# Change of phase in a one-core graph layer: key maximum, returning key rows and weight splits moved around the last tile

## The reference, cut to what matters

```python
xn = layernorm(x)
# graph part: msg[e] = (xn[src[e]] @ W[rel[e]]) * norm[e], summed by dst
# attention part, linear: k is softmaxed over the nodes
k = softmax(xn @ Wk, axis=nodes);  context[h] = k[h].T @ v[h];  out = q @ context
gate = sigmoid(gelu(LN(xn) @ Wg1 + bg1) @ Wg2 + bg2)
x = x + graph + (out * gate) @ Wproj + bproj
# mixture of experts: router, top 2 of 8, w1, gelu, w2
x = x + moe(layernorm(x))
```

## Time and profile before

| | us |
|---|---|
| median of 3 runs | 1686.28 (1685.11 to 1686.80) |
| the profiled execution | 1684.39 |
| its span in the trace | 1682.7 |
| PE busy | 1600.7 (95% of the span) |
| DVE, ACT, POOL busy | 1342.4, 964.2, 1007.7 |

### The profile page before, as it was taken

How to read it: one execution, slowest core, us unless ns; L and a number is a source line. 1 busy time by engine, 2 the same in 40 slices (tenths; PEclk the granted TensorE clock), 3 DMA queues, 4 the chain that set the end, 5 groups by cost and what they waited for, 6 DMA issues and landing times.

```text
span 1682.7 us, 31746 instructions
## 1 busy us (share of the span) xinstructions
PE 1600.7 (95%) x10509; PEld 1449.3 (86%) x10509; DVE 1342.4 (80%) x3389; ACT 964.2 (57%) x2156; POOL 1007.7 (60%) x1111
## 2 busy tenths in 40 slices
PE   7999999899899999998789999999999999999998
PEld 6888888778787777877689999999999999999998
DVE  7888565577677777776569999999999999999985
ACT  4444322345455554554566667667666767676764
POOL 4533322767666667664766766666767767776730
PEclk9999999999999999999899999999999999999999
DMA  9776656677677777778633333333333333333320
GB/s 302 262 259 244 235 226 238 222 250 247 226 254 258 245 240 242 252 240 294 209 95 101 105 102 112 101 108 101 116 102 105 101 115 100 107 99 114 104 62 10
DMA packets 127076, 290.50 MB, mean 173 GB/s; under 512 B 21271, under 2 KB 49724, under 8 KB 126914
## 3 DMA queue, kind: packets, MB, share of 16 engines
q1 hardware_dynamic: 86068, 177.19, 28.9%
q0 software_dynamic: 39952, 110.13, 23.7%
q10 hardware_dynamic: 894, 1.16, 0.2%
HBM read 149.49 MB, written 138.90 MB: 171 GB/s over the span
## 4 chain that ended last, share of the span: by engine, by line
PE 61%; DVE 13%; ACT 8%; issue 8%; another core or an unknown queue 5%; POOL 3%; DMA 1%; DVEq 0%; POOLq 0%; ACTq 0%
PE bank L1805 47%; DVE ml L1590 3%; ACT mh L1026 2%; PE bank L2008 2%; PE bank L1849 2%; DVE xres L1720 2%; DVE ht L1706 2%; POOL raw L691 2%; PE bank L1850 2%; PE bank L2009 2%; ACT raw L1082 2%; PE bank L1860 1%; PE bank L1960 1%; POOL stg L809 1%
## 5 line engine op out<-in xcount | busy, mean ns | idle before, releaser
L809 POOL DMA_INDIRECT stg<-table,idxcur x495 | 538.6, 1088 | 257.0 <-issue 179.4
L1805 PE MATMUL bank<-wreg,xt 128*128 128x512 f32 x2352 | 589.1, 400 | 8.3 <-issue 7.5
L1805 PEld LDWEIGHTS bank<-wreg,xt 128*128 128x128 f32 x2352 | 437.7, 191 | 101.3 <-issue 12.0
L691 POOL DMA_INDIRECT raw<-table,idxa x297 | 304.4, 1025 | 147.9 <-issue 90.1
L1805 PE MATMUL bank<-tt,wreg 128*128 128x256 f32 (+1 forms) x2400 | 318.6, 282 | 1.2 <-DVE tt L1656 1.2
L1805 PE MATMUL bank<-wreg,ht 128*128 128x256 f32 x2352 | 314.7, 282 | 0.5 <-DVE ht L1706 0.2
L1805 PEld LDWEIGHTS bank<-tt,wreg 128*128 128x128 f32 x2400 | 295.6, 189 | 4.2 <-issue 1.5
L1805 PEld LDWEIGHTS bank<-wreg,ht 128*128 128x128 f32 x2352 | 292.6, 188 | 1.7 <-issue 0.8
L1082 ACT ACTIVATE raw<-bank,cols 128x256 f32<-128x256 f32 (+1 forms) x400 | 164.9, 464 | 122.7 <-remote 70.8
L1219 DVE COPY stg<-bank 128x512 f32<-128x512 f32 x196 | 134.5, 687 | 126.1 <-PE bank L1805 88.1
L1590 DVE SCALAR_TENSOR_TENSOR ml<-stg,nrm,mh 128x256 fp32r<-128x256 f32 x455 | 196.0, 480 | 13.8 <-ACT mh L1026 13.8
(11 more groups left out here) (244 smaller groups left out, 2159.6 us busy)
## 6 DMA issues: line engine op xcount, KB each, us to landing
table<-stg SPq DMA_DIRECT2D x196, 512.0 KB
kv_d<-kvs SPq DMA_DIRECT2D x49, 256.5 KB
xt_d<-xt SPq DMA_DIRECT2D x49, 256.0 KB
xtp<-xt_d SPq DMA_DIRECT2D x24, 512.0 KB
stg<-table,idxcur POOLq DMA_INDIRECT x495
sk<-kv_d SPq DMA_DIRECT2D x24, 256.5 KB
out_x<-xres SPq DMA_DIRECT2D x24, 256.0 KB
xres<-in_x POOLq DMA_DIRECT2D x23, 256.0 KB, 3.8
```

The lines of the kernel that those rows point to most:

```text
L691: pool.indirect_dma_start(ring_a[:, r * EARLY + j, :], None, table[0:LIMIT, :], bass.IndirectOffsetOnAxis(ap=idxa[:, at:at + 1], axis=0)). ...
L809: pool.indirect_dma_start(stg[:, (s % 4) * SUP + j, :], None, table, bass.IndirectOffsetOnAxis(ap=idxcur[:, at:at + 1], axis=0)).then_inc( ...
L1805: mm = pe.matmul(dst, stat(a, c), mov(b, c), start=(n == 0), stop=(n == 3 * chunks - 1))
```

## The change

Six things change, all around tile 48 and pairs 0 and 1.

1. The turning, reducing and spreading of the key maximum is moved into tile 48 (`last_maximum` on DVE, a transpose at j = 7 on PE). The held tiles are shifted and exponentiated ahead of `first_phase_over`.
2. Parts 2 to 5 of the returning rows are loaded by SP in the middle of tile 48's stores; `later` then covers relation matrices already read. The parts are used in the order 2, 3, 4, 5, 0, 1, three of them in slot 0.
3. `wreg` is laid out by chunks, HI and LO of a chunk side by side, and chunks 4 and 5 go to the two places that `later` does not cover (`place_of`).
4. The chunks are split in slots (0,2), (0,3), (0,6), (0,7) by ACT and (0,3), (0,4), (0,7), (1,1) by DVE; before it was (0,7), (1,0), (1,2), (1,3) and (0,7), (1,0), (1,4), (1,5).
5. The end of the context is moved from slots 5 and 6 of pair 0 to slots 3 and 4. `OUT` and `GATES` of the first output pair move to the end of slot (0,7), and the rest of that pair's steps come one slot earlier in pair 1 (`SLOTS_OF_SECOND`).
6. The experts' products wait for the weight chunk that they read, in place of one wait for all.

```diff
+        weights = sb("wreg", [P, 4, 2, CC, WC, C], F32R)
+        wreg = weights[:].rearrange("p n h c r o -> p h n c r o")
...
+        def place_of(n):
+            return n if n < 4 else (n + 2) % 4
...
             def stores(k, i, b):
...
+                    if at(k, NT - 1) and h < 2:
+                        if h == 0:
+                            sp.wait_ge(kv_st[0], 16 * (NP + 1))
+                            sp.wait_ge(kv_st[1], 16 * NP)
+                        sp.wait_ge(gnn_mm, 8 * k + 2 * h + 2)
+                        load_rows(2 + 2 * h)
+                        load_rows(3 + 2 * h)
...
             load_rows(0)
             load_rows(1)
             first_phase_over(sp)
-            for part in range(2, 2 * GROUPS):
-                load_rows(part)
...
-                if (i, s) == SPLITS[0]:
+                if (i, s) == SPLITS[2]:
                     act.wait_ge(ctx_mm, HELD + REST)
...
+            def last_maximum():
+                dve.wait_ge(setup_pe, 4)
+                dve.wait_ge(gnn_mm, 8 * (NT - 1))
+                dve.wait_ge(xt_st[1], 16 * NP)
+                ch.link(dve, dve.tensor_reduce(kcol, bank[1][:, 0:C].rearrange("p (c n) -> p c n", c=CC), AX.X, ALU.max))
+                for c in range(CC):
+                    dve.tensor_scalar(dg[:, c * P:(c + 1) * P], ident[:], kcol[:, c:c + 1], None,
+                                      ALU.mult).then_inc(k_shift_diag, 1)
+            def held_shifts():
+                dve.wait_ge(kv_st[0], 16 * (NP + 1))
+                dve.wait_ge(kv_st[1], 16 * NP)
+                for b in range(HELD):
+                    dve.tensor_tensor(kvs[b][:, 0:C], kvs[b][:, 0:C], dg[:], ALU.subtract).then_inc(k_shift, 1)
...
+            dve.wait_ge(kmb_mm, 1)
+            ch.link(dve, dve.tensor_copy(dg[:], bank[1][:, C:2 * C]))
+            held_shifts()
+            dve.tensor_tensor(fade, kcol1, kcol, ALU.subtract).then_inc(k1_dve, 1)
+            keep_contexts(NT - 1, NP, 0, 7)
+            keep_contexts(NT - 1, NP, 1, 0)
             dve.wait_ge(flag_ready, 1)
             far = dve.value_load(flag[0:1, 0:1], min_val=0, max_val=NT * P * R)
             first_phase_over(dve)
...
+                    if at(k, NT - 1) and j == 7:
+                        pe.wait_ge(kmax_up, NT)
+                        for c in range(CC):
+                            mm = pe.transpose(bank[1][:, c * P:(c + 1) * P], kmax[:, c * P:(c + 1) * P], ident[:])
+                        mm.then_inc(setup_pe, 1)
...
-                if isinstance(i, int) and (i, s) == (0, 5):
+                if isinstance(i, int) and (i, s) == (0, 3):
                     context_turn()
                     context_values()
-                if isinstance(i, int) and (i, s) == (0, 6):
+                if isinstance(i, int) and (i, s) == (0, 4):
                     query_context()
+                if isinstance(i, int) and (i, s) == (0, 7):
+                    OUT(0, 2)
+                    GATES(0, 2)
...
-PARTS_OF_SLOT = {0: (0, 1), 1: (2,), 2: (3,), 3: (4,), 4: (5,)}
-SPLITS = ((0, 7), (1, 0), (1, 2), (1, 3))
-SPLITS_LOW = ((0, 7), (1, 0), (1, 4), (1, 5))
+PART_ORDER = (2, 3, 4, 5, 0, 1)
+PARTS_OF_SLOT = {0: (2, 3, 4), 1: (5,), 2: (0,), 3: (1,)}
+SPLITS = ((0, 2), (0, 3), (0, 6), (0, 7))
+SPLITS_LOW = ((0, 3), (0, 4), (0, 7), (1, 1))
```

87 lines of the change are left out of this document (41 added, 46 removed).

## The result

The changed kernel took 1705.89 us, the median of four runs between 1700.16 and 1709.02; the kernel before, beside it, 1686.54. The ratio on record is 1.0091, 95% interval 1.0067 to 1.0115; it is not the quotient of the two medians, which would be 1.0115. The forecast of 1692.8 had the sign right and the size wrong, and the time lies outside its range of 1680 to 1699. The profiled execution took 1700.16, the quickest of the four, its span 1698.5 against 1682.7, so a difference of 15.8 us is what the traces can explain; the medians differ by 19.4.

The account below looks back on a forecast made before the run. PE bounds from pair 2 on; before it, pair 1's first gather and a fixed run of gathers. +8.9 - 2.4 = +6.5 us on the profiled 1684.4 gives 1690.9; the median lies 1.9 higher: 1692.8, range 1680 to 1699.

Parts of the forecast that it names:

- The hg_d store, 785.1 (bounds 782.8 to 786.0): End of tile 48: store behind 4.73 MB of queued loads and table pieces lands at 785.1, against 775.84 before.
- Part 2 on TensorE at 787.9: Behind the store's landing: after shift, exponential and hand-over, TensorE starts part 2 at 787.9, having idled 6.4 us.
- Contexts end at 810.9: Pair 0: returning rows' products and first four groups' sums take 23.0 us, so contexts end at 810.9, against 810.1 before.
- POOL's own start is no bound: Pair 0's gathers begin at about 787 instead of 779.88; twenty take 25 us, ending at 812, so they set nothing.
- a rival had priced at 3.5 to 4.5: Contexts behind TensorE's idle: clock falls to 1.2 GHz, adding 3.5 to 4.5 us, time 1697; chance 0.09.
- The context's chain, 8.1 us ahead of group 4: Slots 3 and 4 of pair 0: turn, copy, split, masking and query product delay group 4's sum by 8.1 us.
- T: Start of pair 1's first gather, 812.32 before; claimed to set the turn's end, with a fixed run of gathers behind it.
- T +8.9: Pair 1's first gather starts at 821.2 instead of 812.3, 8.9 us later, from the contexts' end and the context's chain.
- Splits, -2.4 behind T: Pair 1: two of four weight splits no longer lie beside its gathers, saving 2.4 us.
- The output steps one slot earlier free nothing: Pair 1: output steps moved a slot earlier gain nothing, since the sums wait for gathers; priced at zero.
- The rival of the stall: Pair 2's start: unexplained TensorE stretch of single products goes, 7.7 us saved, time 1685.1; chance 0.20 alone.
- That the queue does not hold: Tile 48: hg_d store and pieces land as before, phase over at 776.5, time 1686.4; chance 0.11 alone.

Follow-up runs that it names:

- e7: Changed kernel with tile 48's last hg_d store issued from ScalarE's DMA queue instead of SyncE's; ratio 1.0103 to the kernel before.
- e9b: Changed kernel with 34 unread products (17 calls) in TensorE's idle time behind the held tiles' products; ratio 1.0121 to the kernel before.
- e1: Changed kernel with the fourteen loads of the later rows put directly behind tile 48's stores; ratio 1.0047 to the kernel before.
- h1: Changed kernel with loads behind tile 48's stores and pair 1's steps in the old slots, context's end and splits still early; ratio 1.0066 to the kernel before.
- f2: Changed kernel with loads behind the stores, context's end back in slots 5 and 6, pair 1's steps in the old slots; 1601.93 us, ratio 1.0003 to before.
- f1: Changed kernel with loads behind the stores, context's end back in slots 5 and 6, weights' splits back in their old slots; ratio 1.0056 to before.
- e5: Changed kernel with loads behind the stores and context's end back behind group 4's sum, second table kept; 1605.21 us, ratio 1.0049 to the kernel before.
- g1: Changed kernel with POOL's roots of pair 1's statistics ahead of slot 5's gathers instead of slot 6's; ratio 1.0074 to the kernel before.
- g2: Changed kernel with pair 1's first two experts' products, logits and their followers one slot later; ratio 1.0077 to the kernel before.
- e0: Changed kernel run again unaltered, in the faster group of sets; ratio 1.0101 to the kernel before.

## Why the prediction was wrong

Three terms of the sum failed: the landing of the hg_d store and the stretch of the contexts were priced too low, and the second table of slots was put at nothing.

- **The hg_d store, 785.1 (bounds 782.8 to 786.0): the first failed step, 2.1 us too early.** It was seen at 787.24, +11.4 and not +9.3. The sum priced only bytes in the queue and took SyncE's issues for no bound. But the loads' fourteen issues (8.48 us) stood ahead of this one. Of the 11.4 us, 6.5 are the later issue and 4.9 the longer way from issue to landing (7.8 for 2.9). Order within the queue, my reason for the delay, goes with 1.9 us of the latter (e7).
- **Part 2 on TensorE at 787.9: 789.95**, idle 8.84 and not 6.4. This is the term above handed on.
- **Contexts end at 810.9: the second failed step, and the largest miss.** They ended at 816.3. Of the 5.4 us, 2.05 are the late start just named and 3.3 a longer stretch, 26.3 us for the 23.0 of products that the forecast took. It wrote that POOL's own start is no bound, with gathers at about 787 that end at 812. The first gather started at 791.78, the first rows were there at 800.83, and ScalarE, TensorE's sums and the last part of the later rows stood behind them (8.43 us of wait). Two things hold this stretch at once. e9b takes the half clock away, and the contexts' end moves by 0.8 us only. e7 has the later rows' products start 4.2 us sooner but not the gather, and the contexts end no sooner. e1 moves both, these products by 4.7 us and the gather by 12, and the contexts end 6 sooner, though the 44 products still take 12.07 us there. The 2.5 us of clock that a rival had priced at 3.5 to 4.5 are there, and lie under the wait for the gather.
- **The context's chain, 8.1 us ahead of group 4: right, with some luck.** From the contexts' end to T it took 10.6 us (826.87 - 816.29) where the forecast had 10.3 (821.2 - 810.9). Inside it two misses of a microsecond cancel: the turn started 0.9 us behind the contexts and not 1.9, and the query product took 2.07 us and not 1.05. h1 against f2 shows the chain as a price on the time.
- **T +8.9: +14.6**, of which 6.0 are the contexts' end (forecast 0.8) and 8.5 the chain (8.1).
- **Splits, -2.4 behind T: a gain that was paid for ahead of T** (f1). The forecast counted both, the 2.28 us inside its 8.1; the net is nothing.
- **"The output steps one slot earlier free nothing": the third failed step.** I looked only at whether the sums would gain, and priced the second table at nothing without asking what is queued behind the moved steps. Statistics a slot earlier wait on POOL's list for roots behind the gathers of slot 6 (6.18 us on DVE, 2.72 on TensorE), and the first experts' product brings a table load and a Gelu ahead of ScalarE's messages (2.63). f2 against e5 puts the table at 3 to 7 us; which of the two waits costs how much of it is not separated (g1, g2). No rival named it.
- **The rival of the stall was right as to the trace**: 9.1 us became 2.6. From T to pair 2's second output product both traces have the same 51 us, the table's waits in the one for the stall in the other. So the gain of 7.7 us did not show in T plus this stretch. The profile alone would have acquitted the table; it took f2 against e5, in the group without the stall, to see its price.
- **That the queue does not hold** was wrong: the store came late. Its reason, a store that overtakes the loads in its own queue, was not borne out: 7.8 us passed from its issue to its landing.

With the parts that failed put in, 6.5 + 5.2 (contexts' end, 6.0 for 0.8) + 0.4 (chain) + 2.4 (splits) + 1.3 (T to the end) give 15.8, the profiled difference. This is bookkeeping between two traces, not a test of the single parts: the 1.3 (T to the end of the span took 870.4 us before and 871.6 after) hold the table, the splits and the stall together.

Open is what the loads cost. By the ratios of group 2 the chain alone costs 0.63% and the table alone 0.46%, on top of f2, while both with the loads make no more than 0.98% (1.0101 for 1.0003). Counted from the transpose to the end, one trace each, the chain is 5.3 us, the table 4.3 and all three 11.4, which leaves 1.8 for the loads; in group 1, with both others in place, the loads are 6.4 us in the traces (926.8 and 920.4) and 0.44% in the ratio. Open too is what the single products are: nothing in these traces shows what feeds TensorE there. If the changed kernel were simply rid of the 7.7 us of stall in group 1, its ratios in the two groups should be 0.46% apart; they are 1.0091 and 1.0101.

## What to carry to other kernels

Ask of each transfer put ahead in a queue who waits for the last one behind it: here the gathers' table pieces, not the small store that "ends the phase". A step moved to an earlier slot is priced by what then stands behind it in each engine's list, a GpSimd list with fixed places above all. And where one step starts the pipeline that the others follow, here the first gather, shortening another engine's path beside it brought nothing, even with the clock regained.

## What the runs showed of the hardware

- A store of 128 rows that took 1.9 us ahead of the loads (e1) took 6.7 us in a queue of its own beside them (e7, at 302 GB/s between 722 and 728.6), and 7.8 to 8.6 behind them in their queue (changed kernel, and e0 at 400 GB/s between 720 and 733).
- GpSimd's two selects and two copies took 1.26 us alone and 3.97 beside VectorE's shifts with two SBUF inputs; one indirect gather took 4.32 us for 0.95 beside a split.
- TensorE gave 44 products of 257 columns in 12.3 us behind 7.5 us of idle time and in 9.8 with the idle time filled (e0, e9b); the granted clock was 0.50 in the first 4 us of the former and 1.00 in the latter.
- The same kernel ran in two groups of sets 5% apart (1598 and 1686 us for the kernel before), more than any edit here. In the slower group TensorE had 21 to 37 us of idle time that nothing in the trace ends, in the faster group 0 to 1.4. Only ratios within a set can be compared.
